# A feed-forward kernel on one core: the head of the first batch rebuilt, with another order of all engines

## Chip, cores and metric

One core of one Trainium2 chip. The time is that of one execution in device microseconds. The median of three runs of the kernel before is 1354.47 us (1354.02 to 1354.80).

## What is computed

For each of 8 batches, x has 1024 tokens of 512 values. A reaction and diffusion step gives y; a two-layer network with a low-rank term of its own for each batch is applied to y, and x is added.

```python
lap_x = yp_x[:, :, :-2] - 2.0 * x + yp_x[:, :, 2:]      # along the 512 values, reflected ends
lap_y = yp_y[:, :-2, :] - 2.0 * x + yp_y[:, 2:, :]      # along the 1024 tokens
y = zX * lap_x + zY * lap_y + zR * x * (1.0 - x)
lt = y[:, 1:17]; even = lt[:, ::2]; odd = lt[:, 1::2]   # 8 even and 8 odd rows
m1 = (even[:, :4, :, None] * odd[:, :4, None, :]).reshape(8, 2048, 512)
m2 = (even[:, 4:, :, None] * odd[:, 4:, None, :]).reshape(8, 512, 2048)
h = gelu(y @ W1.T + scale * (y @ m1.T) + b1)
out = x + h @ W2.T + scale * (h @ m2.T) + b2
```

## The kernel before

y is kept with its values on the partitions, as eight tiles of 4 x 128 partitions-and-blocks by 128 tokens: y1 holds tokens 0 to 511 (tiles 0 to 3), y2 the rest (tiles 4 to 7). W1 and W2 are folded with their batch's outer product (W1 + scale m1), so that the low-rank terms cost no products. The 2048 hidden values are 16 tiles of 128, taken as 8 pairs i. Each operand of a product is split into a high and a low part (W1h, W1l, yh, yl, gh, gl, W2h, W2l), and three products of 128x128 by 128x512 take the place of one in fp32.

Layer 1 goes in two halves of 512 tokens, h = 0 and 1. A pair by Strassen's scheme costs seven block products instead of eight, of 2 x 3 matmuls each: 30 in the first half and 12 in the second. A plain pair costs 24 and 24. Before, pair 0 of batch 0 is plain and all other 63 are Strassen's. Strassen pairs need sums of parts of y (sum1 to sum4, the parts S1, S2, S4, S3) over both halves, sums of W1 blocks on GpSimd (`top0`, `top1`, `top3` into Ts), and additions on PSUM (`c11`, `c22`, `c21`) with copies that ScalarE takes (`cpP`, `cpU`, `cpV`) and that pass through DRAM (UV). Layer 2 adds into the four banks po: for each pair an early and a late hidden tile, 12 products each, one pair behind layer 1.

Every engine has one queue, and its order is written out by hand; semaphores join them. SyncE issues plain transfers and GpSimd those that add on the way (`add_W1` adds W1 from DRAM to the outer product that ScalarE's `outer` has put into R1; `add_b2` adds the bias). VectorE folds W2 (`fold`, four operations of 128x128), makes the low parts (`part_l`, `w1lB`, `w1lT`, `w1lQ`, `w2l`, `glE`, `glL`), finishes tiles of y for the next batch (`mul`, `fin`, `tile`), and adds the result to x (`ev`). ScalarE makes the high parts (`part_h`, `w1hB`, `w2h`, `ghE`, `ghL`) and the gelus.

The head is the part before the first product (line 569). The small vectors come in four transfers: zt (coefficients), zn (the same for 64 partitions), XS (the odd rows' surroundings), b1t. The even rows are computed from N, rows of x in natural layout on 64 partitions, by ten operations on VectorE, ScalarE and GpSimd (lines 1167 to 1180), and written to DRAM twice (EP, EQ), from where EB1 and EB2 are read as broadcasts. y of batch 0 is computed from the eight loads x0. For tiles 0, 1, 2, 4, 5 and 7 TensorE applies the stencil with diagonal matrices DG in fp32 (`sums`, line 562: five matmuls of 512 columns, or three where GpSimd has added neighbours), and VectorE's `tile0` adds the square; tiles 3 and 6 go by `mul`, `fin`, `tile`. All eight tiles and six stencils stand ahead of the first product of layer 1. One row matmul (line 614) broadcasts an even row of W1's pair 0, and VectorE folds it (line 1190).

```python
            sums(5, ph[1], 0, 5).then_inc(s_sten, 1)
            e.wait_ge(s_w1lB, 1)
            e.wait_ge(s_yl[0], 1)
            product(ph[2], 0, 0, 0, True)
```

From batch 1 on the loop over pairs is the same for each batch; the tiles of y of batch b + 1 are made while batch b runs, and W1, W2 and the parts of batch b + 1 are made ready in the second half of batch b.

## Time and profile before

| | |
|---|---|
| median of 3 runs | 1354.47 us |
| the profiled execution | 1355.36 us |
| its span, first to last instruction | 1353.6 us |
| TensorE, matmuls busy | 1340.6 us, 5840 records |
| VectorE busy | 1042.3 us |
| ScalarE busy | 802.7 us |
| GpSimd busy | 423.1 us |
| DMA, bytes read and written | 193.80 and 67.11 MB |

PE is TensorE, DVE is VectorE, ACT is ScalarE, POOL is GpSimd and SP is SyncE. Matmuls overlap, so the time from one's start to the next's, not the duration of one, is what a matmul costs.

### The profile page before, as it was taken

The page shows a single profiled execution, that of the slowest core. Times are in us where ns is not written, and L with a number is a line of the kernel's source. Part 1 is how long each engine was busy: PE and PEld are TensorE (multiplying, and loading weights), DVE is VectorE, ACT ScalarE, POOL GpSimd, SP SyncE. Part 2 cuts the span into 40 slices and gives each one's busy share as a digit, 9 for nine tenths or more (in the row PEclk, how much of TensorE's full clock was granted, in tenths as well). Part 3 has the DMA queues.
Part 4 walks back from the last instruction along what each step waited for, and adds up shares of the span by engine and source line. Part 5 has one row for each costly group of instructions (what it writes and reads, how often), then busy time and mean ns, then how long its engine had stood idle before and what let it go on. Part 6 is the DMA issues. An engine that isn't in the chain of part 4 may idle for free.

```text
span 1353.6 us, 17089 instructions
## 1 busy us (share of the span) xinstructions
PE 1340.6 (99%) x5840; PEld 1096.2 (81%) x5840; DVE 1042.3 (77%) x1676; ACT 802.7 (59%) x1396; POOL 423.1 (31%) x399
## 2 busy tenths in 40 slices
PE   8999999999999999999999999999999999999999
PEld 3778888888888888888888888888878888888887
DVE  6999779958799587985889768896688967675343
ACT  3766467745676456764567556675466754666432
POOL 4452134511454015450245302453125520222100
PEclk9999999999999999999999999999999999999999
DMA  6778768867687677776778758687677866676661
GB/s 194 172 189 242 217 175 216 205 181 210 191 214 215 181 202 201 204 201 212 200 192 202 198 183 211 194 223 182 219 185 191 217 180 212 152 195 164 179 188 54
DMA packets 134071, 262.05 MB, mean 194 GB/s; under 512 B 15200, under 2 KB 23520, under 8 KB 133984
## 3 DMA queue, kind: packets, MB, share of 16 engines
q1 hardware_dynamic: 116104, 209.96, 48.7%
q0 software_dynamic: 17520, 49.81, 22.7%
q10 hardware_dynamic: 360, 1.19, 0.3%
q8 instruction: 46, 0.75, 0.2%
q14 instruction: 41, 0.34, 0.1%
HBM read 193.80 MB, written 67.11 MB: 193 GB/s over the span
## 4 chain that ended last, share of the span: by engine, by line
PE 94%; DVE 4%; issue 1%; DMA 1%; ACT 0%; POOL 0%; SPq 0%; DVEq 0%; ACTq 0%
PE po L579 16%; PE po L580 16%; PE po L581 16%; PE ph L569 15%; PE ph L571 14%; PE ph L573 14%; PE po L562 1%; DVE W2s L1098 1%; DMA zn<-in_z_dram 1%; PE ph L562 1%; DVE y L1089 0%; DVE yl L1068 0%; DVE W2l L1106 0%; DVE y L1085 0%; POOL s L441 0%
## 5 line engine op out<-in xcount | busy, mean ns | idle before, releaser
L579 PE MATMUL po<-W2h,gh 128*128 128x512 f32 x1024 | 398.8, 389 | 3.1 <-DVE gl L1148 3.1
L581 PE MATMUL po<-W2h,gl 128*128 128x512 f32 x1024 | 398.5, 389 | 0.0
L580 PE MATMUL po<-W2l,gh 128*128 128x512 f32 x1024 | 398.4, 389 | 0.0
L569 PE MATMUL ph<-yh,W1h 128*128 128x512 f32 x898 | 351.0, 391 | 2.1 <-DVE ph L1138 1.4
L573 PE MATMUL ph<-yh,W1l 128*128 128x512 f32 x898 | 349.9, 390 | 0.0
L571 PE MATMUL ph<-yl,W1h 128*128 128x512 f32 x898 | 349.9, 390 | 0.0
L579 PEld LDWEIGHTS po<-W2h,gh 128*128 128x128 f32 x1024 | 192.4, 188 | 43.7 <-DVE gl L1148 3.8
L581 PEld LDWEIGHTS po<-W2h,gl 128*128 128x128 f32 x1024 | 192.3, 188 | 40.0
L580 PEld LDWEIGHTS po<-W2l,gh 128*128 128x128 f32 x1024 | 192.4, 188 | 39.7
L569 PEld LDWEIGHTS ph<-yh,W1h 128*128 128x128 f32 x898 | 168.8, 188 | 39.8 <-DVE ph L1138 3.4
L1098 DVE SCALAR_TENSOR_TENSOR W2s<-EB,SC,W2s 128x128 f32<-128x128 f32 x512 | 198.9, 437 | 2.7 <-DMA W2s<-in_w_dram 2.7
L573 PEld LDWEIGHTS ph<-yh,W1l 128*128 128x128 f32 x898 | 168.9, 188 | 35.2
L571 PEld LDWEIGHTS ph<-yl,W1h 128*128 128x128 f32 x898 | 168.9, 188 | 35.0 <-issue 0.2
L460 POOL TENSOR_TENSOR Ts<-R 128x512 f32<-128x512 f32 x63 | 87.2, 1384 | 324.1 <-DVE W1l L1117 284.9
L1148 DVE TENSOR_TENSOR gl<-ph,gh 128x512 fp32r<-128x512 f32 x128 | 87.8, 686 | 100.2 <-ACT gh L809 100.0
L441 POOL TENSOR_TENSOR SS<-X 128x512 f32<-128x512 f32 x56 | 75.9, 1356 | 278.9 <-DMA X<-in_xT_dram 211.1
L1153 DVE TENSOR_TENSOR gl<-ph,gh 128x512 fp32r<-128x512 f32 x128 | 87.3, 682 | 85.8 <-ACT gh L816 85.5
L802 ACT ACTIVATE ph<-ph,b1t 128x512 f32<-128x512 f32 x128 | 84.1, 657 | 71.9 <-DVE ph L1144 70.3
L766 ACT ACTIVATE W2h<-W2s 128x512 fp32r<-128x512 f32 x128 | 80.2, 627 | 61.5 <-DVE W2s L1098 60.9
L1106 DVE TENSOR_TENSOR W2l<-W2s,W2h 128x512 fp32r<-128x512 f32 x128 | 115.5, 902 | 1.6 <-ACT W2h L766 1.6
L735 ACT ACTIVATE R<-EB,SC 128x256 f32<-128x256 f32 x252 | 107.0, 496 | 7.0 <-DVE W1l L1207 3.8
L809 ACT ACTIVATE gh<-ph 128x512 fp32r<-128x512 f32 x128 | 76.6, 599 | 47.6 <-PE po L581 43.4
(92 smaller groups left out, 1482.6 us busy)
## 6 DMA issues: line engine op xcount, KB each, us to landing
W2s<-in_w_dram SPq DMA_DIRECT2D x128, 256.0 KB, 3.3
R<-in_w_dram POOLq DMA_DIRECT2D x63, 512.0 KB, 7.6
uv_scratch<-UVs SPq DMA_DIRECT2D x126, 256.0 KB, 4.5
UVs<-uv_scratch SPq DMA_DIRECT2D x126, 256.0 KB, 3.8
X<-in_xT_dram SPq DMA_DIRECT2D x56, 390.0 KB, 4.6
xr<-in_x_dram SPq DMA_DIRECT2D x16, 1024.0 KB, 5.5
xr<-in_b_dram POOLq DMA_DIRECT2D x16, 1024.0 KB, 11.0
out_dram<-xr SPq DMA_DIRECT2D x64, 256.0 KB, 2.2
```

The costliest lines, as they stand in the source:

```text
L460: e.tensor_tensor(Ts[:, 0:4:2, :], R1[:, f, 0:1, :].broadcast_to([128, 2, 256]), R1[:, f, 1:3, :], ALU.subtract).then_inc(s_top0, 1)
L569: e.matmul(bank[:, :], W1h[:, f, blk, wc], yh[:, q, c, :], start=first and c == 0, stop=False, skip_group_check=not first)
L571: e.matmul(bank[:, :], W1h[:, f, blk, wc], yl[:, q, c, :], start=False, stop=False, skip_group_check=not first)
L573: mm = e.matmul(bank[:, :], W1l[:, f, blk, wc], yh[:, q, c, :], start=False, stop=c == 1, skip_group_check=not first)
L579: e.matmul(po[t][:, :], gh[:, lt, st], W2h[:, k, :], start=i == 0 and lt == 0, stop=False)
L580: e.matmul(po[t][:, :], gh[:, lt, st], W2l[:, k, :], start=False, stop=False)
L581: return e.matmul(po[t][:, :], gl[:, lt, st], W2h[:, k, :], start=False, stop=i == NI - 1 and lt == 1)
L735: m = e.activation(R1[:, f, 2 * h:2 * h + 2, 128 * c:128 * c + 128], EB1[:, :].rearrange("p (a q) -> p a q", a=2), ACT.Copy, scale=SC[:, b ...
L1098: m = e.scalar_tensor_tensor(W2s[:, s, 128 * a:128 * a + 128], EB2[:, a, :], SC[:, b % 2, ck, 4 + a:5 + a], W2s[:, s, 128 * a:128 * a + 12 ...
L1106: e.tensor_tensor(W2l[:, k, :], W2s[:, n % 2, :], W2h[:, k, :].bitcast(f32), ALU.subtract).then_inc(s_w2l, 1)
L1148: e.tensor_tensor(gl[:, 0, :], bank_of(b, h, i, 0)[:, :], gh[:, 0, :].bitcast(f32), ALU.subtract).then_inc(s_glE, 1)
L1153: e.tensor_tensor(gl[:, 1, :], bank_of(b, h, i, 1)[:, :], gh[:, 1, :].bitcast(f32), ALU.subtract).then_inc(s_glL, 1)
```

## The change

- **Inputs.** zt, zn, XS of batch 0 and b1 come as one array PK of 128 x 160. The rows of x that the even rows need come as `xn`, 128 partitions of 1024 values, each half a row of 256 values with its neighbours. The odd rows' quantities are scaled by `scale` at once, in `scalars`, which also computes the even columns for batch 0 (SA).
- **Even rows.** For the plain pairs of batch 0, TensorE makes the broadcast even row from a matrix of ones and diagonal matrices DE (`diagonals` on ScalarE, `even_row`). The natural layout (`natural`, VectorE) is needed for DRAM alone, and is written once, into EP; EB2 reads four rows of 512 bytes for each partition.
- **Stencil.** TensorE computes only tiles 0 to 3: three matmuls for tile 0, two for each other, on sums that VectorE makes (`tokens0`, `channels0`). Tiles 4 to 7 go by `mul`, `fin`, `tile` during the first pairs.
- **Pairs.** PL = 4 pairs of batch 0 are plain; their first half uses tiles 0 to 3 alone. Pair 0 is computed in fp32 for the first half (`full`, 16 matmuls of 256 columns on the folded W1 itself, no high and low parts). Pair 1's three kinds of terms are ordered by when they are ready (`term`). The folded W1 of the four plain pairs goes to DRAM and returns for the second half (`keep_W1`, `load_W1`).
- **W2 of batch 0.** Tiles 3 to 7 are folded as W1 is: ScalarE writes the outer product (`outer2`), GpSimd issues a transfer that adds W2 (`add_W2`).
- **Order.** The queues of all five engines are written anew for batch 0 and up to the first pair of batch 1. Tiles of y of batch 1 are made from pair 5 of batch 0 on and through its second half. From pair 1 of batch 1 on the order is the old one. The sum S3 of batch 0 is kept in A11, and A21 gets parts of its own (`part_A21`), because the plain pairs' second half uses it.

```diff
+    PL = 4
...
             def load_EB2(b, j):
-                if (b, j) > (0, 0):
+                if (b, j) == (0, 0):
+                    e.wait_ge(d_ep, 16)
+                else:
                     pb, pn = (b, 4 * j - 1) if j else (b - 1, 15)
-                    e.wait_ge(s_w2f, folds(pb, pn))
-                e.dma_start(flat(EB2[:, :, :]), EQ[j, 2 * b + 1:2 * b + 2, :].broadcast_to([128, 512])).then_inc(d_e2, 16)
+                    if by_transfer(pb, pn):
+                        e.wait_ge(s_w2o, pn - 2)
+                        if pn == 3:
+                            e.wait_ge(s_w2f, folds(0, 2))
+                    else:
+                        e.wait_ge(s_w2f, folds(pb, pn))
+                e.dma_start(EB2[:, :, :], bass.AP(EP.tensor, (8 * b + 4) * D + 128 * j,
+                                                  [[0, 128], [D, 4], [1, 128]])).then_inc(d_e2, 16)
...
+            def keep_W1(i):
+                if i < 2:
+                    e.wait_ge(s_fold1, i + 1)
+                    raw = UVs[:, 2 * i:2 * i + 2, :]
+                else:
+                    e.wait_ge(d_r[i % 2], added(0, i))
+                    raw = R1[:, i % 2, :, :].rearrange("p (h a) q -> p h (a q)", h=2)
+                e.dma_start(UV[i].rearrange("h p q -> p h q"), raw).then_inc(d_keep[i], 16)
+
+            def load_W1(i):
+                e.wait_ge(d_keep[i], 16)
+                if i < 2:
+                    e.wait_ge(s_w1lT, strassen(0, 6 + i))
+                else:
+                    e.wait_ge(s_w1lQ, pairs(0, i - 2))
+                e.dma_start(R1[:, i % 2, :, :].rearrange("p (h a) q -> p h (a q)", h=2),
+                            UV[i].rearrange("h p q -> p h q")).then_inc(d_back[i % 2], 16)
...
-            e.dma_start(zt[:, :, :].rearrange("p b i -> p (b i)"), bass.AP(z.tensor, 0, [[0, 128], [1, 32]])).then_inc(d_z, 16)
-            e.dma_start(zn[:, 0:4], bass.AP(z.tensor, 0, [[4, 8], [0, 8], [1, 4]])).then_inc(d_zn, 16)
-            load_XS(0)
-            for n in (3, 1, 6, 4, 5, 7):
+            e.dma_start(PK[:, :], pk).then_inc(d_pk, 16)
+            load_x0(1)
+            load_x0(3)
+            for i in range(2):
+                e.dma_start(UVs[:, 2 * i:2 * i + 2, :].rearrange("p h q -> p (h q)"), w1[i]).then_inc(d_raw[i], 16)
+            load_W2(0, 0)
+            load_W2(0, 1)
+            for n in (5, 6, 7):
                 load_x0(n)
...
             e.wait_ge(s_ep, 1)
-            e.dma_start(EP[:, :], N[:, 0, :]).then_inc(d_ep, 16)
-            e.dma_start(bass.AP(EQ.tensor, 0, [[128, 64], [8192, 4], [1, 128]]), N[:, 0, :]).then_inc(d_ep, 16)
-            load_W2(0, 1)
-            load_W2(0, 0)
-            load_EB1(0, 1)
+            e.dma_start(EP.rearrange("r (h q) -> (r h) q", h=2), even).then_inc(d_ep, 16)
...
+            load_EB1(0, 4)
+            for i in range(3):
+                keep_W1(i)
...
+            keep_W1(3)
...
+            load_EB1(0, 6)
+            store_T(0, 4)
+            load_EB2(0, 2)
+            load_W2(0, 8)
+            load_W2(0, 9)
+            load_EB1(0, 7)
...
+            def add_W2(n):
+                e.wait_ge(s_w2o, n - 2)
+                e.dma_start(W2s[:, n % 2, :], w2[n ^ 1], accum_op=ALU.add).then_inc(d_a[n % 2], 16)
...
+            side(0, 4)
+            token(0, 4)
+            add_W1(0, 2)
+            add_W1(0, 3)
+            side(0, 5)
+            token(0, 5)
...
+            add_W2(3)
...
+            add_W1(0, 4)
+            add_W2(4)
+            add_W2(5)
+            top0(0, 4)
+            add_W1(0, 5)
+            top1(0, 4)
+            add_W2(6)
+            top3(0, 4)
+            add_W2(7)
+            add_W1(0, 6)
+            top0(0, 5)
+            top1(0, 5)
+            top3(0, 5)
...
-            def sums(n, bank, first, last):
-                mid, up, down, left, right = x_at(0, n)
-                st, sd = sums_at(0, n)
-                terms = [(3, mid), (0, sd), (1, st)] if n in (2, 7) else [(0, up), (0, down), (1, left), (1, right), (3, mid)]
-                for a in range(first, min(last, len(terms))):
-                    d, src = terms[a]
-                    mm = e.matmul(four(bank[:, :]), DG[:, d, :], src, start=a == 0, stop=a == len(terms) - 1)
+            def mid0(n, first, last):
+                e.wait_ge(d_x[n], 16)
+                e.wait_ge(s_dg, 3)
+                return e.matmul(four(po[n][:, :]), DG[:, 3, :], x_at(0, n)[0], start=first, stop=last)
+
+            def tokens0(n, first, last):
+                e.wait_ge(s_st[n], 1)
+                return e.matmul(four(po[n][:, :]), DG[:, 1, :], sums_at(0, n)[0], start=first, stop=last)
+
+            def channels0(n, first, last):
+                e.wait_ge(s_sd[n], 1)
+                return e.matmul(four(po[n][:, :]), DG[:, 0, :], sums_at(0, n)[1], start=first, stop=last)
+
+            def even_row(j):
+                for c in range(4):
+                    e.wait_ge(s_de, 4 * j + c + 1)
+                    mm = e.matmul(ph[1 + 2 * j][:, 128 * c:128 * c + 128], ON[:, :], DE[:, j, c, :], start=True, stop=True)
+                mm.then_inc(s_row, 1)
+
+            def full(bank, blk, part, s, first):
+                raw = UVs[:, 0:2, :].rearrange("p h (a q) -> p (h a) q", a=2)
+                for c in range(2):
+                    mm = e.matmul(bank[:, 256 * s:256 * s + 256], raw[:, blk, 128 * c:128 * c + 128],
+                                  part[:, c, 256 * s:256 * s + 256], start=first and c == 0, stop=not first and c == 1)
                 return mm
...
+            def term(bank, w, blk, part, s, first, last):
+                for c in range(2):
+                    mm = e.matmul(bank[:, :], w[:, 1, blk, 128 * c:128 * c + 128], part[:, s, c, :],
+                                  start=first and c == 0, stop=last and c == 1)
+                return mm
...
-            sums(0, po[0], 0, 4)
-            e.wait_ge(s_dg, 2)
-            sums(0, po[0], 4, 5).then_inc(s_sten, 1)
-            e.wait_ge(d_x[1], 16)
-            sums(1, po[1], 0, 5).then_inc(s_sten, 1)
-            e.wait_ge(s_ep, 1)
-            e.wait_ge(s_sel, 2)
-            e.matmul(ph[2][:, 0:256], DG[0:64, 2, :], N[:, 0, 0:256], start=True, stop=True).then_inc(s_row, 1)
-            e.wait_ge(s_mt, at_sum(0, 2))
-            sums(2, po[2], 0, 3).then_inc(s_sten, 1)
-            e.wait_ge(d_x[4], 16)
-            sums(4, po[3], 0, 5).then_inc(s_sten, 1)
-            e.wait_ge(s_mt, at_sum(0, 7))
-            sums(7, ph[3], 0, 3).then_inc(s_sten, 1)
-            e.wait_ge(d_x[5], 16)
-            sums(5, ph[1], 0, 5).then_inc(s_sten, 1)
-
+            mid0(0, True, False)
+            tokens0(0, False, False)
+            channels0(0, False, True).then_inc(s_sten, 1)
+            even_row(0)
+            tokens0(1, True, False)
+            channels0(1, False, True).then_inc(s_sten, 1)
+            tokens0(2, True, False)
+            channels0(2, False, True).then_inc(s_sten, 1)
+            tokens0(3, True, False)
+            channels0(3, False, True).then_inc(s_sten, 1)
+            even_row(1)
+            e.wait_ge(s_fold1, 1)
+            e.wait_ge(s_tile, 2)
+            full(ph[2], 1, A11, 0, True)
+            full(ph[2], 3, A12, 0, False)
+            full(ph[0], 0, A11, 0, True)
+            full(ph[0], 2, A12, 0, False)
+            e.wait_ge(s_tile, 4)
+            full(ph[2], 1, A11, 1, True)
+            full(ph[2], 3, A12, 1, False).then_inc(s_plain, 1)
+            full(ph[0], 0, A11, 1, True)
+            full(ph[0], 2, A12, 1, False).then_inc(s_p3, 1)
+
+            e.wait_ge(s_outer, 2)
+            e.wait_ge(s_yh[0], 1)
+            e.wait_ge(s_yh[1], 1)
+            e.wait_ge(s_w1hB, 1)
+            for bank, lt in ((ph[3], 1), (ph[1], 0)):
+                for s in range(2):
+                    term(bank, W1h, 2 * s + lt, yh0, s, s == 0, False)
             e.wait_ge(s_w1lB, 1)
+            for bank, lt in ((ph[3], 1), (ph[1], 0)):
+                for s in range(2):
+                    term(bank, W1l, 2 * s + lt, yh0, s, False, False)
             e.wait_ge(s_yl[0], 1)
-            product(ph[2], 0, 0, 0, True)
             e.wait_ge(s_yl[1], 1)
-            product(ph[2], 0, 2, 1, False).then_inc(s_plain, 1)
-            e.wait_ge(s_w1lT, 1)
-            product(ph[0], 0, 3, 0, True)
-            product(ph[0], 0, 1, 1, False).then_inc(s_p3, 1)
-
-            past = (0, 0, 0)
+            for bank, lt, done in ((ph[3], 1, s_plain), (ph[1], 0, s_p3)):
+                for s in range(2):
+                    mm = term(bank, W1h, 2 * s + lt, yl0, s, False, s == 1)
+                mm.then_inc(done, 1)
+            for src, w, ready in ((gh, W2h, s_w2h), (gl, W2h, s_glE), (gh, W2l, s_w2l)):
+                e.wait_ge(ready, 1)
+                for t in range(4):
+                    mm = e.matmul(po[t][:, :], src[:, 0, 128 * t:128 * t + 128], w[:, 1, :], start=w is W2h and src is gh,
+                                  stop=False)
+            mm.then_inc(s_l2E, 1)
+            layer2_late(0, 0, 0)
+            for i in range(2, PL):
+                f = i % 2
+                e.wait_ge(s_w1lB, i)
+                product(ph[2 + f], f, 1, 0, True)
+                product(ph[2 + f], f, 3, 1, False).then_inc(s_plain, 1)
+                for t in range(4):
+                    layer2_early(0, 0, i - 1, t)
+                product(ph[f], f, 0, 0, True)
+                product(ph[f], f, 2, 1, False).then_inc(s_p3, 1)
+                layer2_late(0, 0, i - 1)
+
+            past = (0, 0, PL - 1)
...
+            def outer2(n):
+                s, ck = n % 2, (n ^ 1) % 4
+                e.wait_ge(s_w2l, tiles2(0, n - 2))
+                e.wait_ge(d_e2, 16 * (n // 4 + 1))
+                for a in range(4):
+                    m = e.activation(W2s[:, s, 128 * a:128 * a + 128], EB2[:, a, :], ACT.Copy, scale=SC[:, 0, ck, 4 + a:5 + a])
+                m.then_inc(s_w2o, 1)
...
+            def diagonals(j):
+                e.wait_ge(s_sel, 1)
+                e.wait_ge(s_sc, 6)
+                for c in range(4):
+                    e.activation(DE[:, j, c, :], DG[:, 2, :], ACT.Copy, scale=SA[:, c, 2 * j:2 * j + 1]).then_inc(s_de, 1)
...
+            def fold_W1(i):
+                raw = UVs[:, 2 * i:2 * i + 2, :].rearrange("p h (a q) -> p (h a) q", a=2)
+                e.wait_ge(d_raw[i], 16)
+                e.wait_ge(s_row, 1)
+                for cd in range(4):
+                    h, c = divmod(cd, 2)
+                    blk = raw[:, 2 * h:2 * h + 2, 128 * c:128 * c + 128]
+                    m = e.scalar_tensor_tensor(blk, ph[1][:, 256 * i:256 * i + 256].rearrange("p (a q) -> p a q", a=2),
+                                               SC[:, 0, cd, 0:1], blk, ALU.mult, ALU.add)
+                m.then_inc(s_fold1, 1)
+
+            def natural():
+                e.wait_ge(d_N, 16)
+                e.tensor_tensor(nA, nA, nC, ALU.add).then_inc(s_na, 1)
+                e.tensor_tensor(nB, nM[:, 0:256], nM[:, 256:512], ALU.add).then_inc(s_nb, 1)
+                e.wait_ge(s_nw, 1)
+                e.tensor_tensor(nW, nW, nM[:, 128:384], ALU.mult).then_inc(s_nm, 1)
+                e.wait_ge(s_na, 1)
+                e.wait_ge(s_nm, 1)
+                e.scalar_tensor_tensor(nW, nA, zt[:, 8, 1:2], nW, ALU.mult, ALU.add).then_inc(s_nm, 1)
+                e.wait_ge(s_nb, 1)
+                e.wait_ge(s_nm, 2)
+                e.scalar_tensor_tensor(even, nB, zt[:, 8, 0:1], nW, ALU.mult, ALU.add).then_inc(s_ep, 1)
+
+            def w1l_plain(i):
+                raw = UVs[:, 2:4, :].rearrange("p h (a q) -> p (h a) q", a=2) if i == 1 else R1[:, i % 2, :, :]
+                e.wait_ge(s_w1hB, i)
+                e.tensor_tensor(W1l[:, i % 2, 0:4, :], raw, W1h[:, i % 2, 0:4, :].bitcast(f32),
+                                ALU.subtract).then_inc(s_w1lB, 1)
...
+            scalars(0)
+            tokens0(0)
+            channels0(0)
+            tokens0(1)
+            channels0(1)
+            tile0(0)
+            mul(0, 1)
+            tokens0(2)
+            channels0(2)
+            tokens0(3)
+            channels0(3)
+            fold_W1(0)
+            tile0(1)
+            mul(0, 2)
             mul(0, 3)
-            tile0(1, po[1])
-            e.wait_ge(d_raw, 16)
-            e.wait_ge(s_row, 1)
-            for cd in range(4):
-                h, c = divmod(cd, 2)
-                blk = R1[:, 0, 2 * h:2 * h + 2, 128 * c:128 * c + 128]
-                m = e.scalar_tensor_tensor(blk, ph[2][:, 0:256].rearrange("p (a q) -> p a q", a=2), SC[:, 0, cd, 0:1], blk,
-                                           ALU.mult, ALU.add)
-            m.then_inc(s_fold1, 1)
-            tile0(2, po[2])
+            tile0(2)
+            tile0(3)
+            natural()
+            fold_W1(1)
+            part_l(0, 0)
+            w1l_plain(1)
+            part_l(0, 1)
+            glE(0, 0, 0)
+            glL(0, 0, 0)
+            fold(0, 0, 0, 4)
+            fold(0, 1, 0, 4)
+            w2l(0, 0)
+            w2l(0, 1)
```

## Rows read from the trace of the kernel before

**Rows 1.** The page's head and busy times: us, share of the span, instructions.

```profile
span 1353.6 us, 17089 instructions
...
PE 1340.6 (99%) x5840; PEld 1096.2 (81%) x5840; DVE 1042.3 (77%) x1676; ACT 802.7 (59%) x1396; POOL 423.1 (31%) x399
```

**Rows 2.** Windows: busy us (count) of each engine, granted TensorE clock, DMA share, GB/s.

```profile
15.00:20.00 5.00, 3.26 (x7) 1.12 (x6) 4.89 (x8) 0.81 (x3) 5.00 (x5) 0.89 0.69 189
20.00:25.00 5.00, 5.00 (x10) 2.15 (x9) 1.74 (x3) 2.08 (x5) 4.01 (x4) 0.77 0.55 198
45.00:50.00 5.00, 4.41 (x12) 3.51 (x13) 5.00 (x10) 3.77 (x8) 2.05 (x2) 0.66 0.13 21
600.00:800.00 200.00, 199.97 (x882) 165.33 (x881) 152.87 (x241) 117.72 (x203) 57.61 (x54) 1.00 0.73 198
```

**Rows 3.** TensorE's timeline: start, duration, line, operation, shapes, count, idle before.

```profile
6.45 4.56 PE L562 MATMUL po<-x,DG 128*128 128x512 f32 x10 [0.94 <-POOL DG L431]
...
16.18 0.70 PE L614 MATMUL ph<-xr,DG 64*128 64x256 f32 x2
18.62 1.83 PE L562 MATMUL po<-x,DG 128*128 128x512 f32 x2 [1.74 <-POOL s L446]
...
22.99 4.46 PE L562 MATMUL po<-x,DG 128*128 128x512 f32 x10
...
33.76 0.80 PE L569 MATMUL ph<-yh,W1h 128*128 128x512 f32 x1
...
45.59 0.50 PE L579 MATMUL po<-W2h,gh 128*128 128x512 f32 x1 [3.06 <-DVE gl L1148]
...
51.41 0.39 PE L569 MATMUL ph<-yh,W1h 128*128 128x512 f32 x1
...
1349.86 0.39 PE L581 MATMUL po<-W2h,gl 128*128 128x512 f32 x1
```

**Rows 4.** TensorE's waits over the span: us in total, times, longest.

```profile
PE po L579 <- DVE gl L1148: 3.1, 1, 3.1
...
PE ph L569 <- DVE ph L1138: 1.4, 2, 1.2
```

**Rows 5.** VectorE's timeline, first 62 us.

```profile
5.24 0.17 DVE L1037 TENSOR_SCALAR zc<-zt 128x8 f32<-128x8 f32 x1 [5.24 <-DMA zt<-in_z_dram]
...
18.25 1.64 DVE L1190 SCALAR_TENSOR_TENSOR R<-ph,SC,R 128x256 f32<-128x256 f32 x4
...
43.12 1.21 DVE L1068 TENSOR_TENSOR yl<-y,yh 128x1024 fp32r<-128x1024 f32 x1
44.25 0.68 DVE L1117 TENSOR_TENSOR W1l<-Ts,W1h 128x512 fp32r<-128x512 f32 x1
44.85 0.68 DVE L1148 TENSOR_TENSOR gl<-ph,gh 128x512 fp32r<-128x512 f32 x1
45.46 1.12 DVE L1098 SCALAR_TENSOR_TENSOR W2s<-EB,SC,W2s 128x128 f32<-128x128 f32 x4
```

**Rows 6.** The page's costliest groups: busy us, mean ns, idle before.

```profile
L1098 DVE SCALAR_TENSOR_TENSOR W2s<-EB,SC,W2s 128x128 f32<-128x128 f32 x512 | 198.9, 437 | 2.7 <-DMA W2s<-in_w_dram 2.7
...
L1148 DVE TENSOR_TENSOR gl<-ph,gh 128x512 fp32r<-128x512 f32 x128 | 87.8, 686 | 100.2 <-ACT gh L809 100.0
...
L766 ACT ACTIVATE W2h<-W2s 128x512 fp32r<-128x512 f32 x128 | 80.2, 627 | 61.5 <-DVE W2s L1098 60.9
L1106 DVE TENSOR_TENSOR W2l<-W2s,W2h 128x512 fp32r<-128x512 f32 x128 | 115.5, 902 | 1.6 <-ACT W2h L766 1.6
L735 ACT ACTIVATE R<-EB,SC 128x256 f32<-128x256 f32 x252 | 107.0, 496 | 7.0 <-DVE W1l L1207 3.8
```

**Rows 7.** DMA issues of the first 40 us: count, KB, median us to landing.

```profile
R<-in_w_dram POOLq DMA_DIRECT2D x2, 512.0 KB, 6.7
...
EB<-eq_scratch SPq DMA_DIRECT2D x1, 256.0 KB, 4.9
...
ep_scratch<-xr SPq DMA_DIRECT2D x1, 128.0 KB, 2.3
```

1273 lines of the change are left out of this document (719 added, 554 removed).

## The prediction

> **What bounds the kernel now.** The busy times come first [rows 1]: TensorE works 1340.6 of 1353.6 us. No other engine can set the time of the whole, only of stretches. The windows [rows 2] give the pace: 882 products in 200 us, 0.2268 us each, and that is a floor for one 512-column product. Layer 2 has 3072 of them. Layer 1 of before has 48 for the plain pair and 42 for each of 63 Strassen pairs, 2694. So 5766 x 0.2268 = 1307.7 us is bought before any wait. The rest, 46 us, is the head, the waits and the tail.
>
> TensorE's timeline [rows 3] shows the head. The first product of layer 1 starts at 33.76; before it lie 26 stencil matmuls in fp32, at 4.46 us for 10 records, that is 0.86 us for each matmul of two records. After 36 products TensorE waits 3.1 us for gl [rows 4], and runs slowly after it. At 51.41 it has done 54 products, 5712 remain, and from here it hardly stops: 5712 x 0.2268 = 1295.5 takes it to 1346.9, and the last starts at 1349.86, ends at 1350.25. So all that goes wrong after 51.4 is 3.3 us, 1.4 of it waits for the Strassen sums [rows 4]; the tail is 3.35 us. The profiled execution took 1355.36 us, 1.76 more than its span and 0.9 more than the median of 1354.47. I subtract a gain from the median.
>
> So the question is when the new head reaches the same point, 5712 products left, and whether the helpers keep up from there.
>
> **TensorE's work.** The new layer 1 of batch 0 has 16 fp32 matmuls of 256 columns (pair 0, first half), 24 (pair 0, second half), 3 x 48 and 4 x 42 products, 336 of the usual kind. Pair 0, pair 1 and layer 2 of pair 0 are done when 5760 - 48 = 5712 remain: the same count as at 51.41. The four plain pairs cost 3 x 6 products more, 4.1 us, and this stands in the count already.
>
> **The new head, step by step.** One transfer, PK, replaces zt, zn, XS and b1t for this stage. zt, of 16 KB, let VectorE start at 5.24 [rows 5]; PK has 80 KB but goes first. Bounds: 4.7 and 6.5; I take 5.2. The four zc operations and the seven small ones of `scalars` take 2.4 us (before, the four took about 0.8). Then VectorE adds the neighbours of tile 0: a 128x512 addition starts every 0.60 us, a 128x1024 one every 1.13 [rows 5], so both sums are there at 8.85. TensorE's channels0(0) is the third fp32 matmul and ends about 10.15.
> - even_row(0), four matmuls of 128 columns, two records each. By columns 0.9 us, by 0.227 a record 1.8; the nearest row, two records in 0.70 [rows 3], is nearer the second. 1.7, to 11.9.
> - Six stencil matmuls of tiles 1 to 3 at 0.86: 5.2, to 17.1. The VectorE sums come at 10.05, 12.85 and 14.05, and are not waited for.
> - even_row(1): 1.7, to 18.8.
> - 16 fp32 matmuls of 256 columns: 0.43 by columns, 0.454 by records, 7.3, to 26.1. VectorE must have W1 folded and tiles 0 to 3 done: fold_W1(0) (four from PSUM took 1.64 [rows 5]) ends at 15.7, tile 3 at 18.85. Both in time.
> - Pair 1: 24 x 0.227 = 5.4, to 31.5. VectorE: `natural` (five operations of 256 columns in 128 partitions, about half of the 0.60 and more of one of 512, with their waits) 2.1 to 20.9, fold_W1(1) to 22.5, a part_l, w1l_plain(1) after ScalarE's rounding (25.3) to 26.4, the second part_l to 27.6. ScalarE is pushed by even_row(1): two `outer` at 4 x 0.43 from 18.8, two part_h, then w1h_plain(1) to 25.3. The high parts go first, so TensorE finds each operand.
> - Layer 2 of pair 0: 24 x 0.227 = 5.4, to 36.9. The even row reaches DRAM and returns as EB2 with 0.5 + 2.3 + 0.4 + 4.9 us [rows 7] after 20.9, at 29.0; two folds of four (1.12 each, clean) and w2l end at 31.7 and 32.3; the first is wanted at 33.3. Cover: 1.6 us. Without it each us late is a us of TensorE.
>
> So 36.9 against 51.41 if the clock stays up. It did not before: windows at 0.89, 0.77 and 0.66 [rows 2] follow waits of 1.74 and 3.06 us [rows 3]. Part of each was on the lower of its two levels, 1.2 GHz. A window of 5 us at 0.66 has lost 1.7 us of the full clock, and so has the pair at 0.89 and 0.77. The new head has waits of about 1 us at 5.5 and 7.4 and small ones on VectorE. I put one such fall on the path: 38.6. Bounds: none and three, 36.9 and 42.0. Gain up to here 51.4 - 38.6 = 12.8.
>
> The Trainium skill ("TensorE: Matmul & The Clock Gate", What's actually happening) says that the slow level is the default and that activity lifts it; by that a head with many short waits could stay slow longer, which is the fourth rival's case.
>
> **What is given back.** First, tiles 3 to 7 of W2 take a detour: ScalarE writes the outer product (`outer2`, four of 128 columns, about 1.3 us by [rows 6]), GpSimd issues an adding transfer, then w2h and w2l. The nearest transfer is R's, 6.7 us for 512 KB [rows 7]; 256 KB should take 4 to 6.7, I take 5. One round of a slot is 1.3 + 0.9 + 5 + 0.6 + 0.7 = 8.5, two slots run side by side, and TensorE takes 48 x 0.227 = 10.9 us over the two tiles of a plain pair. Following the queues from 32 us, I find w2l(0,4) some 0.5 us ahead of TensorE, w2l(0,5) and w1lB(0,4) also within 1. EB2 for tile 4 is issued only after fold(0,2), about 36, and lands 4.9 us later, holding ScalarE's whole queue (gelu, gh) behind outer2(4). Price: from 0 to 6; I take 1.5.
>
> VectorE is freed there of five folds (5 x 1.06), and pays for tiles 4 to 7 with three operations each (1.9 against one of 0.65). Where GpSimd works beside it, operations with both inputs in SBUF stretch: w2l has a mean of 0.902 us against 0.68 clean, a fold 0.437 against 0.28, while gl, whose input is in PSUM, stays at 0.686 [rows 5, 6].
>
> Second, the seam of batch 0 and 1. Batch 1's y tiles now wait until the second half of batch 0. From w1lQ(0,5) through the first pair of batch 1 I count 45.1 us of clean VectorE work, in 4 x 36 x 0.227 + 54 x 0.227 = 44.9 us of TensorE. Stretched by the share that the rows give (about 1.16) it is 52, but the last folds and tile operations are not wanted at once and GpSimd has little to do there. Bounds 0 and 7; I take 1.5. The four pairs before have room (some 6 us of 10.9).
>
> EB2 is read in pieces of 512 bytes instead of 2 KB, 32 times; it is asked for a step ahead after the head, so I cost it at nothing, at most 1 us each where the head waits. UV as a keep for four W1 blocks moves bytes off the path. The later batches keep their order: nothing, and their 1.4 us of waits stay.
>
> Sum: 12.8 - 1.5 - 1.5 = 9.8; 1354.47 - 9.8 = 1344.7 us (on its own execution 1355.4 - 9.8 = 1345.6, a span near 1343.8).
>
> **Rivals.**
> 1. Nothing is given back and no fall of the clock lies on the path: gain 14.5, 1340.0. For it: TensorE found operands ready in each step above. Against: margins under 1 us at three places.
> 2. VectorE at the seam is the bound: 52 against 44.9 us, 7 lost instead of 1.5, 1350.2. For it: the clean work alone fills the stretch. Against: the smaller of the two waits for the Strassen sums [rows 4], 0.2 us, is all that the old seam cost.
> 3. The other side: the W2 detour serializes. If ScalarE's and GpSimd's queues let only one slot's round run at a time, two tiles take 17 to 23 us instead of 10.9, over two and a half pairs 15 to 30 us. It decides from about 5 us a pair on; at 8 a pair it costs 20, gain 12.8 - 20 = -7, 1361.7. For it: each adding transfer stands behind others in GpSimd's queue, and outer2 behind gelus. Against: outer2(4) and outer2(5) follow each other.
> 4. The clock: two more falls of 1.7 us in the head, 1348.1. For it: [rows 2]; against: TensorE has dense work from 10 us on.
>
> The rule named above would make this one likelier; by the rows it took waits of 1.7 us and more.
>
> **How the numbers follow.** Forecast 0.52, rival 1 0.15, rival 2 0.12, rival 4 0.10, rival 3 0.07; 0.04 that the detour or a late PK eats the gain to within 2.7 us. That is 0.2% of the time, about what a measurement of this kernel can tell from no change. Faster: 0.52 + 0.15 + 0.12 + 0.10 = 0.89, less 0.01 for rival 2 with a fall of the clock: 0.88; same 0.04; slower 0.08. The range from 1338 (rival 1 with PK 0.5 us early and even_row at its lower bound) to 1351.5 (rival 2 and a little) leaves out rival 3 and thin ends, 2 in 10.
>
> **What would show it.** The first 256-column fp32 matmul near 19 us and the last before 27; the first layer 2 product near 31 to 33; VectorE in `natural` near 19 to 21. Wrong would be: a granted clock under 0.8 over more than 10 us of the head; TensorE waiting for W2l between 45 and 60; TensorE waiting for gl, W1l or the Strassen sums from 150 to 200 us; a pace other than 882 products per 200 us in later batches.

## Result and the profile after

The changed kernel takes 1364.08 us (median of 4 runs, 1363.54 to 1369.52), the kernel before 1354.24 in the same session: ratio 1.0078, 95% interval 1.0063 to 1.0093. It is slower by 0.8%; forecast were 1344.7 us and 0.7% faster. The profiled execution took 1364.42 us.

The page's head, then windows (columns as in [rows 2]):

```profile
span 1362.7 us, 17128 instructions
...
PE 1339.2 (98%) x5846; PEld 1098.3 (81%) x5846; DVE 1042.0 (76%) x1664; ACT 805.9 (59%) x1407; POOL 415.9 (31%) x393
```

```profile
15.00:20.00 5.00, 5.00 (x27) 4.31 (x26) 4.79 (x10) 3.45 (x9) 2.18 (x3) 1.00 0.19 76
20.00:25.00 5.00, 5.00 (x24) 4.17 (x22) 5.00 (x7) 4.68 (x7) 3.05 (x3) 1.00 1.01 193
...
40.00:45.00 5.00, 4.42 (x12) 3.51 (x13) 4.88 (x7) 3.10 (x8) 0.00 (x0) 0.66 0.61 146
80.00:90.00 10.00, 7.94 (x29) 6.11 (x28) 10.00 (x17) 4.42 (x9) 4.92 (x5) 0.83 0.60 155
110.00:120.00 10.00, 6.45 (x23) 4.92 (x22) 4.34 (x8) 4.63 (x7) 2.29 (x2) 0.83 0.82 233
187.90:246.40 58.50, 49.47 (x202) 38.03 (x202) 51.79 (x83) 34.83 (x62) 27.12 (x26) 0.97 0.77 196
600.00:800.00 200.00, 198.79 (x878) 164.27 (x877) 155.04 (x248) 119.76 (x207) 61.38 (x57) 1.00 0.72 196
```

TensorE's work is the same as before and so is its pace in later batches: the four products fewer in the last window are one wait of 1.2 us for a Strassen addition, and before has such a wait too, elsewhere. The head is clean: the granted clock, which fell to 0.77 in before [rows 2], is 1.00 in every window of 5 us up to 40 us. What is new are low clocks at 40, 80 and 110 us, and the stretch from 187.9 to 246.4 us, in which 200 products took 58.5 us instead of 45.4. TensorE's timeline (columns as in [rows 3]) gives the head and three of the waits, the list below it the waits over the span:

```profile
9.41 1.05 PE L665 MATMUL ph<-DE,ON 128*128 128x128 f32 x8
10.31 1.02 PE L656 MATMUL po<-s,DG 128*128 128x512 f32 x2
...
16.35 7.07 PE L671 MATMUL ph<-y,UVs 128*128 128x256 f32 x32
23.07 2.19 PE L689 MATMUL ph<-yh,W1h 128*128 128x512 f32 x8
...
30.03 1.20 PE L766 MATMUL po<-W2h,gh 128*128 128x512 f32 x4 [0.78 <-ACT W2h L960]
...
40.58 0.50 PE L695 MATMUL po<-W2h,gh 128*128 128x512 f32 x1 [2.10 <-DVE W2l L1417]
...
84.38 0.47 PE L695 MATMUL po<-W2h,gh 128*128 128x512 f32 x1 [2.06 <-DVE gl L1467]
...
117.01 0.80 PE L679 MATMUL ph<-yh,W1h 128*128 128x512 f32 x1 [3.56 <-ACT UVs L979]
```

```profile
PE ph L679 <- ACT UVs L979: 9.3, 4, 3.6
PE po L695 <- DVE W2l L1417: 2.1, 1, 2.1
PE po L695 <- DVE gl L1467: 2.1, 1, 2.1
PE ph L679 <- ACT UVs L967: 1.9, 2, 1.3
```

The best view of where time goes is one that the profile doesn't print: the start of the product after which M matmul records are left, compared between traces (counted in TensorE's timeline, 5840 records in before, 5846 in after and its variants; the moment that [rows 3] shows at 51.41 is the start of the product behind that one). The last column is the result of the whole, by medians:

```
M left            5712   5600   5450   5350   5100   4900   4350
before, us        51.2   76.6  111.7  134.4  191.7  237.1  361.7
after, us         35.4   64.8  103.1  131.0  187.9  246.4  371.1
after - before   -15.8  -11.8   -8.6   -3.4   -3.8   +9.3   +9.3   (+9.8)
```

So the head won more than forecast and everything behind it lost: 4.0 us by 65, 3.2 by 103 and 5.2 by 131 us, all in batch 0's pairs behind the head, and 13.1 (12.7 from M = 5350 on) in the seam of batches 0 and 1. From there on the lag stays between +9.1 and +10.6.

VectorE's timeline at the seam shows three things that the prediction had not: operations that last several times their clean time, folds that wait for W2, and batch 1's Strassen sums at 170.68 us, which in before began at 148.41:

```profile
170.68 1.23 DVE L1384 TENSOR_TENSOR xr<-y 128x1024 f32<-128x1024 f32 x1
...
185.75 4.47 DVE L1417 TENSOR_TENSOR W2l<-W2s,W2h 128x512 fp32r<-128x512 f32 x1
...
201.69 3.99 DVE L1409 SCALAR_TENSOR_TENSOR W2s<-EB,SC,W2s 128x128 f32<-128x128 f32 x4
...
216.63 1.14 DVE L1409 SCALAR_TENSOR_TENSOR W2s<-EB,SC,W2s 128x128 f32<-128x128 f32 x4 [2.29 <-DMA W2s<-in_w_dram]
```

```profile
184.80 1.30 POOL L558 DMA_DIRECT2D xr<-in_b_dram  x1 [12.75 <-DMA xr<-in_x_dram]
185.58 1.84 POOL L516 TENSOR_TENSOR SS<-X 128x512 f32<-128x512 f32 x1
186.95 1.46 POOL L525 TENSOR_TENSOR SS<-X 128x512 f32<-128x512 f32 x1
187.95 1.71 POOL L541 TENSOR_TENSOR Ts<-R 128x512 f32<-128x512 f32 x1
```

The second fence is GpSimd's timeline beside the 4.47 us operation: two stencil sums for tile 0 of batch 2 and a W1 sum, behind the issue of an adding transfer. The w2l ends at 190.22, 0.56 us after these three. The 3.99 us are another case: four folds of 0.34, 1.37, 1.13 and 1.38 us, which took turns with GpSimd's operations.

TensorE's waits at the seam are mostly for ScalarE's copies (line 979), and these lead back to VectorE: ScalarE takes its queue in order, and w2h, which stands ahead of the copy, waited for a fold. The longest one, on VectorE, ScalarE and TensorE in turn, and ScalarE's waits of that kind from 180 to 250 us:

```profile
211.08 1.13 DVE L1409 SCALAR_TENSOR_TENSOR W2s<-EB,SC,W2s 128x128 f32<-128x128 f32 x4
212.24 0.63 ACT L960 ACTIVATE W2h<-W2s 128x512 fp32r<-128x512 f32 x1 [3.58 <-DVE W2s L1409]
213.30 0.58 ACT L979 ACTIVATE UVs<-ph 128x512 f32<-128x512 f32 x1
214.02 0.47 PE L679 MATMUL ph<-yh,W1h 128*128 128x512 f32 x1 [3.11 <-ACT UVs L979]
```

```profile
ACT W2h L960 <- DVE W2s L1409: 17.1, 7, 4.5
```

### The profile page after: what moved, and what is told of

The parts are those of the page before. It is cut to its first block, busy times and chain, and to the rows that moved or that the text cites. A ratio compares the mean times of both kernels' runs of the same rounds, so it can differ in the third digit from the quotient of the medians.

```text
span 1362.7 us, 17128 instructions
## 1 busy us (share of the span) xinstructions
PE 1339.2 (98%) x5846; PEld 1098.3 (81%) x5846; DVE 1042.0 (76%) x1664; ACT 805.9 (59%) x1407; POOL 415.9 (31%) x393
## 4 chain that ended last, share of the span: by engine, by line
PE 88%; DVE 7%; DMA 3%; issue 2%; ACT 1%; SPq 0%; DVEq 0%; ACTq 0%
PE po L695 16%; PE po L696 16%; PE po L697 16%; PE ph L679 14%; PE ph L681 14%; PE ph L683 14%; DVE W2s L1409 1%; DMA W2s<-in_w_dram 1%; DMA R<-uv_scratch 1%; DVE W2l L1417 1%; DVE yl L1375 1%; DVE y L1358 0%; DVE xr L1474 0%; DVE gl L1462 0%; DMA ep_scratch<-SS 0%
## 5 line engine op out<-in xcount | busy, mean ns | idle before, releaser
L696 PEld LDWEIGHTS po<-W2l,gh 128*128 128x128 f32 x1020 | 192.2, 188 | 39.7
L1409 DVE SCALAR_TENSOR_TENSOR W2s<-EB,SC,W2s 128x128 f32<-128x128 f32 x492 | 183.0, 423 | 5.4 <-DMA W2s<-in_w_dram 4.9
L541 POOL TENSOR_TENSOR Ts<-R 128x512 f32<-128x512 f32 x60 | 82.0, 1366 | 285.9 <-DVE W1l L1428 258.5
L1417 DVE TENSOR_TENSOR W2l<-W2s,W2h 128x512 fp32r<-128x512 f32 x128 | 124.5, 973 | 5.0 <-ACT W2h L960 4.7
L999 ACT ACTIVATE ph<-ph,PK 128x512 f32<-128x512 f32 x128 | 84.0, 657 | 74.7 <-DVE ph L1458 71.0
L902 ACT ACTIVATE R<-EB,SC 128x256 f32<-128x256 f32 x240 | 101.9, 498 | 1.5 <-DMA EB<-ep_scratch 1.5
## 6 DMA issues: line engine op xcount, KB each, us to landing
xr<-in_b_dram POOLq DMA_DIRECT2D x16, 1024.0 KB, 10.7
```

Source lines behind the costliest of these rows:

```text
L696: e.matmul(po[t][:, :], gh[:, lt, st], W2l[:, k, :], start=False, stop=False)
L902: m = e.activation(R1[:, f, 2 * h:2 * h + 2, 128 * c:128 * c + 128], row.rearrange("p (a q) -> p a q", a=2), ACT.Copy, scale=SC[:, b % 2, ...
L999: e.activation(bank[:, :], bank[:, :], ACT.Gelu, bias=b1t[:, k:k + 1]).then_inc(s_actL, 1)
L1409: m = e.scalar_tensor_tensor(W2s[:, s, 128 * a:128 * a + 128], EB2[:, a, :], SC[:, b % 2, ck, 4 + a:5 + a], W2s[:, s, 128 * a:128 * a + 12 ...
L1417: e.tensor_tensor(W2l[:, k, :], W2s[:, n % 2, :], W2h[:, k, :].bitcast(f32), ALU.subtract).then_inc(s_w2l, 1)
```

## Experiments

Seventeen kernels. All compute the whole unless it says otherwise. In the expectations "5050 left" (also 5400, 5600) was counted in windows of 2 us, which count a record that crosses an edge twice; by starts it is M = 4900 (about 5200, 5360). Ratios are to before, measured beside it on the same chip. "Lag" is the time at M less before's, from the one profiled execution, which lies up to 4 us from its kernel's median (6.4 in e10), so differences of a us or two between lags of two kernels can be chance.

**One edit at a time, at each wait.** e1 puts GpSimd's stencil sum of tile 6 behind the W2 transfer and a wait, e2 the sums of batch 1's tile 0 behind the W1 sums of pair 6:

```diff
-            token(0, 6)
             add_W2(3)
+            e.wait_ge(s_w2l, 3)
+            token(0, 6)
             side(0, 7)
...
             add_W1(0, 7)
-            side(1, 0)
-            token(1, 0)
             top0(0, 6)
             top1(0, 6)
             top3(0, 6)
+            e.wait_ge(s_glL, 5)
+            side(1, 0)
+            token(1, 0)
```

> The changed kernel, but GpSimd's token sums of tile 6 and both sums of tile 7 wait until VectorE has w2l(0,2); the adding transfer for tile 3 of W2 goes ahead of them. In the changed kernel one mul and one fin of VectorE took 1.53 and 3.11 us beside these sums, and TensorE then waited 2.1 us for W2l at 40.6. Theory H (hold: a VectorE operation with both inputs in SBUF that starts beside a string of GpSimd operations lasts until the string pauses): mul and fin take 0.7 us each, the 2.1 us wait and the slow clock behind it go, the span is 3 to 4 us shorter, near 1359. Rival W (work: VectorE has simply too much to do there): the same stretching falls on the operations that come later, and the span stays within 1 us of 1362.7.

> The changed kernel, but GpSimd does the sums of W1 pair 6 first and side and token of (1,0) only after glL(0,0,4). In the changed kernel one w2l took 4.02 us beside a string of six GpSimd operations from 76.95 to 84.2, and TensorE waited 2.06 us for gl. Theory H: this w2l lasts only until the shorter string ends, about 2.5 us, the wait goes or falls under 0.5, the span is 2 to 3.5 us shorter. Rival W: the string's work moves to other VectorE operations, TensorE waits the same within 0.5 us elsewhere, the span stays within 1 us.

e1: 1363.41 us, ratio 1.0064 (1.0048 to 1.0080). The wait at 40.6 is gone (lag -13.4 at M = 5650, after -11.8), and 11 us later TensorE waits 1.8 us for the next W2l, whose adding transfer took 6.2 us to land: lag -11.8 at 5600, the same as in after. e2: 1362.76, 1.0060 (1.0045 to 1.0076); lag -10.6 at 5500 (after -8.6) and -4.6 at 5350 (after -3.4), but -3.7 at 5100 and +9.4 at 4900, as in after (-3.8 and +9.3). Neither total is clearly below that of after, and neither span fell by the 2 to 4 us that theory H gave.

e3 puts the return of W1's pair 0 ahead of an x load and its rounding behind W2's; e4 puts two W2 loads of the seam ahead of the x loads:

```diff
                 if i == 6:
+                    load_W1(0)
                     load_X(1, 2)
...
-                else:
-                    w1hQ(0, 0)
-                    part_A21()
                 cpV(0, i)
                 gelu_E(0, 0, i)
                 ghE(0, 0, i)
                 w2h(0, 2 * i + 1)
+                if i == 7:
+                    w1hQ(0, 0)
+                    part_A21()
... (e4)
             load_EB2(1, 1)
+            load_W2(1, 5)
             load_X(2, 2)
```

> The changed kernel, but the return of W1 pair 0 is issued ahead of load_X(1,2), and ScalarE and VectorE do w1hQ(0,0), part_A21 and w1lQ(0,0) at the end of pair 7 instead of ahead of cpV(0,7) and glE(0,0,7). Theory Q (queue order: the 10.3 us landing of this transfer stood in front of work that did not need it): the 3.56 us wait at 117 goes, with the slow clock behind it, the span is 4 to 5 us shorter, near 1358. Rival W: VectorE or the transfer is late anyway for the first plain pair of the second half, TensorE waits 3 us a few us later, and the span gains under 1.5 us.

> The changed kernel, but at the start of batch 1 SyncE issues load_W2(1,5) and load_W2(1,7) ahead of load_X(2,2) and load_X(2,3). In the changed kernel VectorE waited 2.3 and 2.6 us for these two loads, and TensorE lost some 12 us between 180 and 250. Theory Q: both waits go, the waits of TensorE at 214, 229.6 and 235 fall by 4 to 5 us together, the span is 4 to 7 us shorter. Rival W: VectorE's work bounds the stretch, it fills the freed time with work that it is behind with, but TensorE's waits fall by less than 2 us.

e3: 1366.27, 1.0097 (1.0072 to 1.0122), slower than after. The copy at 117 us comes in time (lag -9.6 at 5400), but the last W2 tile now lands 9.8 us after its issue and TensorE waits 5.3 us for A21's low part at 119. The theory that the order was to blame fell: the delay moved to another transfer. e4: 1364.24, 1.0070 (1.0055 to 1.0086). Both waits for W2 are gone and nothing is won: VectorE is busy 49.3 of the 50 us from 200 to 250, where it was 44.8 in after. So the loads were not the seam's bound.

**What fills the seam.** e5 leaves out, for batch 2's tiles 0 to 2, all but 16 of 512 columns of GpSimd's sums and of VectorE's mul, fin and tile; e6 of GpSimd's sums alone. Their outputs lack that part.

```diff
+                if (b, n) in ((2, 0), (2, 1), (2, 2)):
+                    sd, up, down = sd[:, :, 0:4], up[:, :, 0:4], down[:, :, 0:4]
                 e.tensor_tensor(sd, up, down, ALU.add).then_inc(s_md, 1)
```

> Leaves work out: for tiles 0, 1 and 2 of batch 2, which fall into the seam of batches 0 and 1, GpSimd's two sums and VectorE's three operations (mul, fin, tile) are done on 16 of 512 columns, so batch 2's even tokens in these tiles are not what the reference has; TensorE's, ScalarE's and all DMA work is as in the kernel after. Yardstick: the moment at which 5050 matmul records are left to do, 238.2 us in before and 246.0 us in after, and in the three versions run so far 245.7 to 246.4 although they came to 5400 left between 2.6 us later and 1.5 us earlier. Theory W, which says that the work of VectorE (nine operations of 0.72 us here, 6.5 us, and what GpSimd's strings add to them) sets the end of the seam: 5050 left by 238 to 241 us, total 1356 to 1359 us. Rival D, which says that the seam waits for transfers (W2 tiles that land 7 us after their issue) or for ScalarE: at most 1.5 us earlier, total 1362 us or more.

> Leaves work out: only GpSimd's two sums of tiles 0, 1 and 2 of batch 2 are done on 16 of 512 columns; VectorE has every operation of the kernel after. Theory H, which says that a VectorE operation with both inputs in SBUF lasts until a string of GpSimd operations beside it ends: w2l at 185.8 us (4.47 us) and the four folds at 201.7 us (3.99 us) come to under 2.5 us each, 5050 left 2 to 5 us earlier than 246.0, total 1359 to 1362 us. Rival, that VectorE's number of operations alone counts: these durations stay within 0.5 us, nothing gained. If this run gains as much as the one that leaves VectorE's work out too, the hold is the whole cause at the seam; if under a third of it, VectorE's own work is.

e5: 1357.25 (1.0016; 1.0006 to 1.0026), e6: 1358.42 (1.0023; 1.0009 to 1.0037). By the medians, six short GpSimd operations bring 5.7 us, and taking nine VectorE operations out besides only 1.2 more, which the intervals don't tell from nothing. In the profiled executions M = 5100 to 4900 costs 13.1 us in after, 9.4 in e6 and 7.4 in e5, and in e6 the w2l of 4.47 us takes 1.23. Both say that for these tiles VectorE loses more time to GpSimd's sums than to its own operations. (e6's profiled execution had no long wait at 117, lag -8.2 at 5350 without an edit there, and its ten runs lie from 1352.84 to 1362.05: that wait varies.)

**The cost by itself.** Two small kernels copy x to the output and compute nothing of the reference: twelve VectorE operations in a row, and beside them a string of GpSimd's. e7 uses additions of 128x512, e9 GpSimd's own operations here:

```diff
+        phases = [("two", 0, False), ("two", 1, False), ("two", 2, False), ("two", 4, False), ("two", 8, False),
+                  ("psum", 4, False), ("fold", 4, False), ("one", 4, False), ("two", 4, True)]
... (VectorE, "two", j = 0 to 11)
+                        m = e.tensor_tensor(c[:, j, :], a[:, :], b[:, :], ALU.subtract)
... (GpSimd, after VectorE's second)
+                    m = e.tensor_tensor(g2[:, j, :], g0[:, :], g1[:, :], ALU.add)
```

> The disputed cost by itself, with none of the reference's computation (the output is a copy of x): VectorE runs twelve operations of 128x512 back to back, and after its second GpSimd begins a string of 0, 1, 2, 4 or 8 additions of 128x512 from SBUF. Theory H: with both inputs in SBUF one of VectorE's operations lasts as long as the whole string, about 1, 2, 4 and 8 times one addition of GpSimd (some 1.0 us), and the others stay at 0.68 us; with one input in PSUM none is longer than 0.7 us; a string that is broken by waits holds back one operation by no more than one addition. Rival, shared bandwidth: every VectorE operation beside the string is longer by the same share (0.68 to 1.0 us or so), and none lasts as long as the string.

> The disputed cost by itself again, with GpSimd's own operations of this kernel (the output is a copy of x, nothing of the reference is computed). In the plain test before, each addition of GpSimd held one VectorE operation back by 1.06 us and the two took turns, so that no operation was longer than 1.75 us, while the kernel's trace has single ones of 4.0 and 4.5 us. Theory H2, that the form of GpSimd's operands (four strided rows of X, a broadcast row of R) lets it go on without giving VectorE a turn: beside the four stencil sums or beside the string sum, sum, top, top, top one operation of VectorE lasts 3 to 5 us. Theory H3, that the issue of an adding transfer by GpSimd (1.3 us for the 1 MB one at 184.8 us) is what holds VectorE: it shows beside the three transfers alone, and beside the string that begins with one, and not beside the string without. Rival, turns as before: no operation over 1.8 us anywhere, and then the long ones of the kernel are several operations of GpSimd that happened to come in a row.

VectorE's timeline of e7, one row for twelve operations (beside 0, 1, 4 and 8 additions; then one of two inputs from PSUM beside 4; then a single input, in SBUF, beside 4):

```profile
7.68 7.32 DVE L85 TENSOR_TENSOR c<-a,b 128x512 f32<-128x512 f32 x12
...
22.33 8.38 DVE L85 TENSOR_TENSOR c<-a,b 128x512 f32<-128x512 f32 x12
...
54.83 11.57 DVE L85 TENSOR_TENSOR c<-a,b 128x512 f32<-128x512 f32 x12
...
73.74 15.83 DVE L85 TENSOR_TENSOR c<-a,b 128x512 f32<-128x512 f32 x12
...
96.91 7.27 DVE L87 TENSOR_TENSOR c<-p,b 128x512 f32<-128x512 f32 x12
...
126.14 8.38 DVE L89 TENSOR_SCALAR c<-a 128x512 f32<-128x512 f32 x12
```

Of the last twelve, those with no addition beside them take less than the others do, so the cost can't be had from the 7.32 above; shortest, median and longest, in ns:

```profile
L89 DVE TENSOR_SCALAR c<-a x12: 413/420/1487, 126.1 to 134.1; 128x512 f32<-128x512 f32 x12
```

The same view of e9: beside sum, sum, top, top, top; beside the issue of the 1 MB transfer alone; beside that issue and the same five. The last row is the summary of the twelve of that third case: shortest, median, longest in ns.

```profile
49.75 11.35 DVE L120 TENSOR_TENSOR c<-a,b 128x512 f32<-128x512 f32 x12
...
97.73 7.31 DVE L120 TENSOR_TENSOR c<-a,b 128x512 f32<-128x512 f32 x12
...
112.38 12.45 DVE L120 TENSOR_TENSOR c<-a,b 128x512 f32<-128x512 f32 x12
```

```profile
L120 DVE TENSOR_TENSOR c<-a,b x12: 679/684/4766, 112.4 to 124.2; 128x512 f32<-128x512 f32 x12
```

Each addition of GpSimd costs VectorE 1.06 us ((8.38 - 7.32), (15.83 - 7.32) / 8), however many there are, and nothing when one of VectorE's two inputs is in PSUM. With a single input, in SBUF, the eight operations with nothing beside them take 0.42 us and the four with an addition 1.48, so the price is the same 1.06 us. Theory H as written for e7 fell: they take turns and no operation exceeds 1.75 us. H2 and H3 fell alone too: the strided sums give turns, and the transfer's issue costs nothing. Only the two together, a string right behind an issue, hold one operation for 4.77 us, through the first three of the five; the other two then take a turn each. The sum over twelve is 5.1 us for five operations, against 4.0 without the issue. So the long operations of the kernel are for the most part the known price in one piece, and which operation pays is decided by where GpSimd's string stands.

**Moving work.** e8 makes batch 1's tiles 5 to 7 earlier, in VectorE's idle time around 143 to 160 us, and its Strassen sums with them. e10 moves batch 2's tiles 1 to 7 into batch 1's pairs 1 to 7:

```diff
             for i in range(1, PL):
                 w1lQ(0, i + 1)
                 glL(0, 1, i - 1)
+                if i > 1:
+                    mul(1, 3 + 2 * (i - 1)); fin(1, 3 + 2 * (i - 1)); tile(1, 3 + 2 * (i - 1))
                 glE(0, 1, i)
-                mul(1, 3 + i); fin(1, 3 + i)
+                if i < 3: mul(1, 2 + 2 * i); fin(1, 2 + 2 * i)
... (e10, VectorE; ScalarE, GpSimd and the x loads accordingly)
-                    if (b, i) == (1, 0):
-                        mul(2, 1); fin(2, 1)
...
-                    if nxt and (b, i) > (1, 0):
+                    if b == 1 and i:
+                        mul(2, i)
+                    elif nxt and b > 1:
                         mul(b + 1, i + 2)
```

> Full computation. Batch 1's stencil tiles 5, 6 and 7 move one to two pairs forward into VectorE's idle time between 134 and 156 us, and with them the Strassen sums of batch 1, which in the kernel after begin at 170.7 us (148.4 us in before); nothing of batch 2 moves. Theory W: sums from about 160 us, no wait of TensorE by 200 us, 5050 left 2 to 5 us earlier than 246.0, total 1359 to 1362 us. Rival D (transfers): at most 1 us. Rival, that an x load which now stands ahead in VectorE's order is late: a wait of gelu's part at 148 to 160 us, and the total is 1364 us or more.

> Full computation. Tiles 1 and 2 of batch 2, with their x loads, their two sums each on GpSimd, ScalarE's scaling and VectorE's three operations, leave the seam; batch 2's tiles 1 to 7 are made one in each of batch 1's pairs 1 to 7 (in the kernel after 1 and 2 in pair 0 and the others in pairs 1 to 5). Theory W with the hold: two of the three tiles whose work cost 5.7 to 6.8 us when it was left out are gone from the seam, 5050 left 3 to 5 us earlier than 246.0, no new wait in pairs 6 and 7 of batch 1 (VectorE is busy 40 of 50 us there), total 1358.5 to 1361 us. Rival: the later tiles make the stretch of pairs 6 and 7 the new bound and the gain is given back by 5 us or more before batch 2, total 1363 us or more.

e8: 1360.24 (1.0046; 1.0032 to 1.0060), as expected. e10: 1368.91 (1.0118; 1.0096 to 1.0140): the rival came true, though not for its reason. I had put GpSimd's sums of a tile one group too early, ahead of the W1 sums that the next pair waits for, and each of them waits 5 to 11 us for its x. e16 below is e10 with this order mended and nothing else: 1357.72, 11.2 us less. e11 and e12 carry the same fault. e12 adds to e11:

```diff
                     load_XS(1)
-                    load_xr(0, 0)
...
                 if i == 6:
                     load_W1(0)
+                if i == 7:
+                    load_X(1, 2)
+                    load_xr(0, 0)
... (GpSimd)
-            add_b2(0, 0)
             side(1, 2)
             token(1, 2)
+            add_b2(0, 0)
```

> Full computation. The two GpSimd orders of the first and second runs (W2 tile 7 and the W1 sums of pair 6 ahead of stencil sums), batch 1's early tiles and batch 2's later tiles together. If the stalls of batch 0's second pairs are given back at the seam only because the seam was bound by VectorE and GpSimd, then with a lighter seam the head's advantage lasts: 5050 left at 236 to 240 us, total 1352 to 1356 us. If each stretch has its own bound (transfers of 6 to 10 us at 104 to 117 us still there): 1356 to 1359 us.

> Full computation. As the run before, and besides the 1 MB load of the residual x at 94 us and the x load of tile 2 go behind the return of W1's first pair and the last W2 tile, and the 1 MB adding transfer of b2 behind tile 2's sums. Theory T, that TensorE's wait at 117 us (3.6 us, for a copy that stood behind a W1 return that landed after 10.3 us) comes from 2 MB of transfers ahead of it: the return lands within 6 us, the wait falls under 1 us, 5600 left 3 us earlier than in the run before, total 1350 to 1354 us. Rival: the return waits for its own turn on SyncE's queue or for W1l, and nothing changes at 117 us; total as in the run before.

e11: 1368.40 (1.0103; 1.0089 to 1.0117). e12: 1362.95 (1.0066; 1.0052 to 1.0079). Between 5450 and 5350 e12 loses nothing (-11.7, -11.7) where e11 loses 7 (-11.7, -4.8). SyncE's queue in e12 and in after, the return of W1 and what stands ahead of it:

```profile
97.65 0.33 SPq L237 DMA_DIRECT2D W2s<-in_w_dram  x1
98.08 0.38 SPq L285 DMA_DIRECT2D R<-uv_scratch  x1
```

```profile
94.05 0.52 SPq L306 DMA_DIRECT2D xr<-in_x_dram  x1
...
103.71 0.33 SPq L205 DMA_DIRECT2D X<-in_xT_dram  x1
104.14 0.38 SPq L285 DMA_DIRECT2D R<-uv_scratch  x1
```

In e12 ScalarE rounds the block at 105.65 without a wait; in after it sits idle for 5.68 us until 114.47, when the return has landed, and the copy that TensorE waits for stands behind it. So theory T has the right place. It doesn't have the right transfer: the 1 MB of x had landed at 102.15, before the return was issued. What stood beside the return was b2's 1 MB adding transfer on GpSimd's queue, which waits for x:

```profile
102.44 1.32 POOL L558 DMA_DIRECT2D xr<-in_b_dram  x1 [4.36 <-DMA xr<-in_x_dram]
```

It landed after 12.2 us and the return, issued 1.7 us behind it, after 10.3. In e12 b2 comes only at 112.92, and the same return lands after 4.3 us; in e3, where it was issued 3.0 us ahead of b2, after 5.9, and the W2 tile that followed b2 after 9.8. The return is also issued earlier, 3.8 us in e13 below, which has this edit alone, since tile 2's x load no longer stands ahead of it. No run moves b2 alone.

**The parts, with the fault mended.** e13 is e12's edit alone; e14 has it, e1, e2 and e8; e15 adds the later tiles, e16 has those alone, e17 those and e8:

```diff
                     if b == 1:
-                        side(2, i + 1)
-                        token(2, i + 1)
+                        if i:
+                            side(2, i)
+                            token(2, i)
```

> Full computation, the kernel after with one edit: the 1 MB load of the residual x and tile 2's x load behind the last W2 load, and the 1 MB adding transfer of b2 behind tile 2's sums. Theory T: TensorE's wait at 117 us (3.6 us) goes, 5600 left at 123 to 125 us (127.8 in after, 133.3 in before). At the seam, which has taken back every earlier gain, 5050 left at 245 to 246 us as in after if VectorE and GpSimd bound it, total 1362 to 1364.5 us; 242 to 243 us and 1360 us if it passes gains on.

> Full computation. The two GpSimd orders, the moved transfers and batch 1's early tiles; batch 2's tiles stay in the seam. 5400 left near 159 us, 13 us ahead of before. Theory W: the seam ends when VectorE and GpSimd have done their work, which starts earlier by the 10 us of batch 1's sums and waits for TensorE's products less: 5050 left at 240 to 243 us, total 1355 to 1359 us. If the seam's end doesn't move with what arrives (as in the runs with one edit): 244 us, 1360 us as with the early tiles alone.

> Full computation. As the run before, with batch 2's tiles 1 to 7 in batch 1's pairs 1 to 7, and GpSimd's sums of a tile now behind the W1 sums of the next pair as in the later batches (in e10 to e12 they stood ahead of them). Theory W: 5050 left at 233 to 236 us (236.3 in e12), no wait over 1.5 us after 225 us, total 1350 to 1354 us, at or below before. Rival: pairs 6 and 7 of batch 1, where VectorE has two tiles more, bound it: 1356 us or more.

> Full computation, the kernel after with one edit: batch 2's tiles 1 to 7 in batch 1's pairs 1 to 7, GpSimd's sums behind the W1 sums of the next pair. Theory W (the seam is bound by VectorE and GpSimd together): 5400 left 6 us ahead of before as in after, 5050 left at 239 to 242 us (246.0 in after), total 1357 to 1360 us, near what leaving that work out gave (1357.3). Rival, that batch 1's late sums alone count: 244 us or later, 1362 us or more.

> Full computation. Both seam edits (batch 1's tiles earlier, batch 2's later), and nothing in batch 0's second pairs. Theory W: what arrives 5 us ahead leaves the seam 1 to 3 us ahead: 5050 left at 235 to 237.5 us, total 1351 to 1354 us, so that the seam accounts for 10 to 13 of the 17 us between the kernel after and e15 and the edits ahead of it for the rest.

```
                                  lag at 5712   5600   5450   5350   5100   4900 | median   ratio (95%)
after                                   -15.8  -11.8   -8.6   -3.4   -3.8   +9.3 | 1364.08  1.0078 (1.0063, 1.0093)
e13 transfers moved                     -15.3  -11.6   -9.4   -9.4   -4.9   +7.6 | 1361.33  1.0047 (1.0030, 1.0065)
e8  batch 1's tiles earlier             -15.8  -11.9   -9.1   -3.8   -4.5   +6.9 | 1360.24  1.0046 (1.0032, 1.0060)
e16 batch 2's tiles later               -16.0  -12.0   -8.7   -3.5   +2.5   +5.8 | 1357.72  1.0019 (1.0009, 1.0028)
e17 both                                -16.0  -12.2   -9.5   -3.8   -4.5   -0.9 | 1353.46  0.9986 (0.9975, 0.9998)
e14 e1 + e2 + e13 + e8                  -16.0  -12.3  -10.3  -10.3   -9.1   +2.0 | 1354.61  1.0002 (0.9993, 1.0010)
e15 all                                 -16.2  -14.0  -12.0  -12.0  -11.8   -8.1 | 1347.16  0.9949 (0.9937, 0.9961)
```

e15 beats both kernels. From M = 5100 to 4900 the seam costs 13.1 us in after, 11.4 with the early tiles and 3.6 to 3.8 with both kinds moved; with the late tiles alone it is 9.3 from M = 5350 on, 6.0 of it before M = 5100. There a low part of y, started behind the issue of b2's second transfer, took 5.71 us instead of 1.22, gl stood behind it, and TensorE waited for gl (VectorE's row and TensorE's, of e16):

```profile
183.02 5.71 DVE L1379 TENSOR_TENSOR yl<-y,yh 128x1024 fp32r<-128x1024 f32 x1
189.39 0.80 PE L700 MATMUL po<-W2h,gh 128*128 128x512 f32 x1 [3.63 <-DVE gl L1471]
```

What arrives earlier is passed on: e14 comes to M = 5100 4.6 us ahead of e8 and leaves the seam 4.9 ahead. e13 shows that a wait moves: the 117 us wait goes, and b2's transfer, now later, makes TensorE wait 2.8 us for the eviction of xr at 130, which e12 and e15 hardly have.

By the medians the parts simply add up. Each one's excess over its own before, less that of after (9.8), gives a gain of 1.7 us for e1, 2.4 for e2, 3.3 for e13, 3.9 for e8 and 6.8 for e16, 18 in all; e15 gained 17.5. e8 and e16 make 10.7, e17 gained 11.0; e1, e2, e13 and e8 make 11.3, e14 gained 10.0. The intervals of e1, e2 and e13 overlap that of after, so each of these three by itself could be nothing; that the edits need each other is not shown.

e15's page head, and the windows of the seam in e15 and in before:

```profile
span 1347.9 us, 17129 instructions
```

```profile
179.90:229.00 49.10, 46.37 (x202) 37.25 (x201) 45.91 (x75) 32.94 (x60) 20.64 (x22) 1.00 0.82 208
```

```profile
191.70:237.10 45.40, 45.40 (x202) 37.58 (x201) 39.74 (x67) 31.88 (x59) 20.40 (x19) 1.00 0.77 205
```

For the same 200 products VectorE was busy 39.7 us in before, 51.8 in after and 45.9 in e15, GpSimd 20.4, 27.1 and 20.6. In after VectorE alone is busy longer than the 45.4 us that TensorE needs, and it was idle for another 6.7 of the 58.5.

## Why the prediction was wrong, step by step

- **TensorE's count and pace**: right; 878 records in 200 us, 882 in before, and the 1.2 us wait accounts for the four; between M = 4900 and the end the lag moves by 1.5 us at most.
- **The head**: right in its order, and the gain too small. VectorE starts at 4.29 (5.2 taken, bounds 4.7 to 6.5), the scalars end at 6.9 (7.6). even_row takes 0.90 us (9.41 to 10.31), its lower bound, where 1.7 was taken: twice 0.8 us. The sixteen fp32 matmuls take 6.7 (7.3). Pair 1 takes 7.0 (23.07 to 30.03) where 5.4 was taken, 0.8 of it a wait for W2h. The point with 5712 left came at 35.4, 15.8 us ahead, not 12.8: the fall of the clock that I put on the path (1.7) didn't happen, and the earlier start and even_row gave the rest. By the rule of the Trainium skill weighed there ("TensorE: Matmul & The Clock Gate", What's actually happening) a head with many short waits could have stayed slow; the windows from 15 to 25 us at 1.00 say no. Rival 4 is out, and of rival 1 the half on the clock was right.
- **"What is given back. First ... I take 1.5"** is the first step that failed: from the head to M = 5350 batch 0 gave back 12.4 us (-15.8 to -3.4). Only a third is the W2 detour (4.0, inside its bounds of 0 to 6). The trace of after puts it down to VectorE's fin, 3.1 us beside GpSimd's sums right behind the issue of add_W2(3); e1 shows that this wait can go and that the next tile's landing of 6.2 us then bounds. The other 8.4 us had no term at all. 3.2 at 84 us: GpSimd's sums for batch 1 ahead of W1's, and VectorE held beside them (e2). 5.2 at 117: "UV as a keep for four W1 blocks moves bytes off the path" was wrong; the 512 KB return was issued behind tile 2's x load and b2's adding transfer and landed after 10.3 us (e12, e13).
- **"Bounds 0 and 7; I take 1.5"** for the seam is the second, and the larger: 13.1 us. I had the work, 45.1 us clean in 44.9, and let two sentences make it harmless. "GpSimd has little to do there" was false: 27.1 us in 26 operations, against 20.4 in 19 before, and e6 shows that six of them cost 5.7 us by the medians, 3.7 of it at the seam in the profiled executions. "The last folds and tile operations are not wanted at once" was true and did not help, since VectorE takes its queue in order, and ScalarE's copies for TensorE stand behind w2h, which waits for the folds. Nor did I see that the order left VectorE idle 17 of 60 us from 120 to 180 while it postponed the sums by 22 us; e8, e16 and e17 show that this, and batch 2's first tiles behind it, are most of the seam's cost: e17 alone wins 11 of the 17.5 us.
- **Rivals.** Rival 2 named the right engine and place and gave 7 us and 1350.2; measured were 13.1. Rival 3 had the right side, slower, and a mechanism that did not happen: the two slots of W2 run side by side (adding transfers issued at 45.24 and 47.11 landed at 49.27 and 51.34). The result is outside the range since I never let both prices be high together. The range should have added the bounds: 6 + 7 and an unknown for the stretch between.
- **The signs of being wrong.** One of them came, and small: TensorE waited 1.2 us for gl at 190.9. Most of the loss at the seam lay behind 200 us, and the first wait for W2l came at 40.6, before the stretch from 45 to 60 that the prediction watched.

What stays open: why the string behind an issue takes VectorE's turns, whether b2's transfer alone makes the return late, and how much of the residual 3.8 us of e15's seam is W2's landing. None of these was tried.

## What to carry to other kernels

When a head gets faster, ask which engine did the work that the old, slow head was hiding, and list what each helper's queue now has between the head and the first steady batch; here 16 us were won in the first 35 and 25 lost in the next 210. Price VectorE in such a stretch as its clean work plus the number of GpSimd's two-input operations times what one costs it, and look for idle time just ahead of a full stretch and work that can wait until behind it: moving work out of the seam both ways (e17, 11 us) was worth more than removing three waits (7 us by their single gains). Three of the five repairs, each measured alone, could not be told from nothing, and all five were worth 17 us; so keep small gains until they can be measured together, and use the lag at fixed points of the work to see where each acts.

## What the runs showed of the hardware

- One GpSimd operation with two SBUF inputs of 128x512 costs VectorE 1.06 us if both of VectorE's inputs are in SBUF ((8.38 - 7.32) and (15.83 - 7.32) / 8 in e7), 1.06 us if it has one input and that in SBUF (1.48 - 0.42), and nothing if one of two is in PSUM (7.27 us for twelve). GpSimd pays as well: 1.65 us instead of 1.23. The Trainium skill ("GPSIMD Engine Reference", Specifications) names contention with VectorE instructions of two SBUF inputs, and the trace agrees.
- Behind the issue of an adding transfer GpSimd's next operations can leave VectorE no turn: one VectorE operation lasted 4.77 us in e9 (through three of GpSimd's), 4.47 and 4.02 in after, 5.71 in e16. The issue alone cost VectorE nothing (7.31 against 7.32 us for twelve).
- A 512 KB load issued 1.7 to 1.9 us behind a 1 MB adding transfer landed after 10.3 (after) and 10.5 us (e13); with no such transfer ahead of it, after 5.9 (e3), 4.3 (e12) and 4.2 us (e13). In e6, only 0.6 us behind one, it took 5.1.
- Eight records of 128 columns in fp32 took 0.90 us, two of 512 columns 0.86, so small fp32 matmuls went by their columns here.
